# Sixteen-head attention scheduled two heads at a time, with the score matmuls of an even and an odd head alternating on the two halves of TensorE's rows

## The reference, cut to what matters

```python
def _L0_attn_b_ref(x, Q, K, V, W):
    q = jnp.einsum('qdh,bcd->bhcq', Q, x) * sq
    k = jnp.einsum('qdh,bcd->bhcq', K, x) * sq
    v = jnp.einsum('vdh,bcd->bhcv', V, x) * sv
    att = jnp.einsum('bhcq,bhCq->bhcC', q, k) / d_query
    att = jnp.where(causal, att, -jnp.inf)
    p = jax.nn.softmax(att, axis=-1)
    y = jnp.einsum('bhcC,bhCv->bhcv', p, v)
    z = jnp.einsum('dvh,bhcv->bcd', W, y) * (math.sqrt(d_embed / d_value) / num_heads)
    return z
...
x = x + _L0_attn_b_ref(_layernorm(x, axis=-1), ...)
x = x + _L0_ffn_ref(_layernorm(x, axis=-1), ...)
```

## Time and profile before

| | |
|---|---|
| time, median of 3 runs | 1553.86 us (1552.02 to 1555.83) |
| the profiled execution: its own time | 1554.59 us |
| its span | 1552.8 us |
| attention B on TensorE | about 444 to 1330 us of the span |
| TensorE busy (matmul) | 1316.0 us, 85% |
| VectorE busy | 1109.7 us, 71% |
| ScalarE busy | 952.8 us, 61% |
| GpSimd busy | 764.5 us, 49% |

### The profile page before, as it was taken

How to read it: one execution, slowest core, us unless ns; L and a number is a source line. 1 busy time by engine, 2 the same in 40 slices (tenths; PEclk the granted TensorE clock), 3 DMA queues, 4 the chain that set the end, 5 groups by cost and what they waited for, 6 DMA issues and landing times. The chain is left out here.

```text
span 1552.8 us, 28434 instructions
## 1 busy us (share of the span) xinstructions
PE 1316.0 (85%) x8377; PEld 1121.1 (72%) x8377; DVE 1109.7 (71%) x2822; ACT 952.8 (61%) x2522; POOL 764.5 (49%) x954
## 2 busy tenths in 40 slices
PE   2676744999849999999999999999999995499990
PEld 1565633888837888888888888888888884388880
DVE  5666434777727788888887888888888874377771
ACT  1555322444427788888788888888887885144440
POOL 3015362444415555576575674765765655244443
PEclk9888556999959999999999999999999997699995
DMA  9391011222100000000000000000000000122215
GB/s 182 131 355 33 25 38 44 57 58 56 36 28 14 1 15 1 2 23 7 1 25 5 5 25 1 22 8 1 11 5 5 11 1 14 37 57 58 56 44 163
DMA packets 91936, 64.47 MB, mean 42 GB/s; under 512 B 34020, under 2 KB 77935, under 8 KB 91792
## 3 DMA queue, kind: packets, MB, share of 16 engines
q1 hardware_dynamic: 83152, 45.75, 10.8%
q0 software_dynamic: 8640, 16.93, 3.4%
HBM read 26.59 MB, written 36.96 MB: 41 GB/s over the span
## 5 line engine op out<-in xcount | busy, mean ns | idle before, releaser
L1359 POOL TENSOR_TENSOR b_probs<-b_probs,b_recip 128x128 f32<-128x128 f32 (+3 forms) x512 | 352.2, 718 | 309.9 <-DVE b_recip L1592 309.9
L420 DVE TENSOR_TENSOR b_pt_lo<-b_ring,b_pt_hi 128x512 fp32r<-128x512 f32 (+1 forms) x384 | 219.0, 598 | 94.0 <-ACT b_pt_hi L414 91.7
L545 ACT ACTIVATE b_probs<-b_s_bank,b_neg_max 128x256 f32<-128x256 f32 (+3 forms) x512 | 267.8, 533 | 28.2 <-DVE b_neg_max L537 26.8
L537 DVE TENSOR_REDUCE b_neg_max<-b_s_bank 128x1 f32<-128x256 f32 (+3 forms) x512 | 219.4, 477 | 48.7 <-PE b_s_bank L529 47.7
L1219 POOL DMA_INDIRECT y_rows<-f_y_sb,f_dest x142 | 138.9, 978 | 215.1 <-DVE f_y_sb L1197 207.7
L414 ACT ACTIVATE b_pt_hi<-b_ring 128x512 fp32r<-128x512 f32 (+1 forms) x384 | 192.1, 547 | 9.6 <-PE b_ring L485 8.8
L81 PE MATMUL b_s_bank<-b_k_hi,b_q_hi 64*128 64x256 f32 (+3 forms) x512 | 180.8, 353 | 2.9 <-ACT b_probs L545 1.4
L485 PE MATMUL b_ring<-ident,b_probs 128*128 128x128 f32 x1280 | 178.6, 277 | 4.6 <-DVE b_q_lo L420 4.4
L82 PE MATMUL b_s_bank<-b_k_lo,b_q_hi 64*128 64x256 f32 (+3 forms) x512 | 164.6, 322 | 0.0
L554 PE MATMUL b_pv_bank<-b_pt_hi,b_v 128*128 128x512 f32 (+3 forms) x512 | 159.2, 322 | 6.3 <-DVE b_y L1555 5.2
L83 PE MATMUL b_s_bank<-b_k_hi,b_q_lo 64*128 64x256 f32 (+3 forms) x512 | 164.0, 320 | 0.0
(11 more groups left out here) (303 smaller groups left out, 3341.0 us busy)
## 6 DMA issues: line engine op xcount, KB each, us to landing
x_sorted<-a_blank SPq DMA_DIRECT2D x64, 260.0 KB, 3.9
f_xs<-x_sorted SPq DMA_DIRECT2D x142, 65.0 KB, 1.8
b_yc<-y_rows SPq DMA_DIRECT2D x16, 256.0 KB, 3.1
f_yc<-y_rows SPq DMA_DIRECT2D x16, 256.0 KB, 3.2
y_rows<-f_y_sb,f_dest POOLq DMA_INDIRECT x142, 2.2
x_tok<-in_L_attn_a_x_dram SPq DMA_DIRECT2D x8, 256.0 KB, 4.5
out_dram<-x_tok SPq DMA_DIRECT2D x8, 256.0 KB, 2.5
f_raw<-in_L_ffn_W_dram SPq DMA_DIRECT2D x1, 1408.0 KB, 6.6
```

The source lines that it names most:

```text
L420: nc.vector.tensor_tensor(dst, src(rg.of(key)), hi.bitcast(F32), ALU.subtract).then_inc(rg.lo_done, 1)
L537: nc.vector.tensor_reduce(sc.neg_max[:, i:i + 1], s_tile(sc, i), AX.X, ALU.max, negate=True).then_inc(sc.max_done, 1)
L545: nc.scalar.activation(probs[:, P_AT[i]:P_AT[i] + (i + 1) * P], s_tile(sc, i), ACT.Exp, bias=sc.neg_max[:, i:i + 1], accum_out=sums[:, i:i ...
L1359: nc.gpsimd.tensor_tensor(part, part, recip[:, i:i + 1].to_broadcast([P, (i + 1) * P]), ALU.mult).then_inc(probs_done, 1)
```

## The change

`attention_b` now counts slots in pairs of heads: p runs over 64 pairs, with eight slots for a sequence. What changes inside:

- **Scores** (`scores(p, group)`): three groups of tiles, (3,), (2, 0) and (1,). In each group the matmuls of the even head (x = 0, rows 0 to 63) and of the odd head (x = 1, rows 64 to 127) alternate, into two different banks of the same three banks, which are handed out round (`s_use` modulo 3). TensorE's other work of the slot stands between the groups.
- **Buffers**: `probs` has three buffers instead of two, `pt`, `neg_max`, `sums` and `recip` have two each (one for each x). To make room, `xn` uses the routing's `xn_t`, `yc` uses `xn_t` and `z`, and `over` and `spread` of the routing lie over other tiles.
- **Order**: on every engine the steps of a slot are put in a new order. The transposes of the even head of pair p − 1 stand right behind the first score group of p; those of the odd head stand before the last group. The division of both heads of p − 1 stands in slot p. The projections of q and k for p + 1 stand behind the last score group in every slot, followed by one set of products alone.
- **Waits**: the exponential of the odd head's first group waits until the even head before it has been transposed (its `probs` buffer is that head's).
- The once-a-sequence steps have new slot numbers, and GpSimd's `rstd` stands ahead of the division in its slot.

What is computed, and the shapes of all matmuls, copies and exponentials, stay as they are. The diff, cut to its core:

```diff
+P_GROUPS = ((3,), (2, 0), (1,))
+P_COL = {3: 0, 2: 0, 0: 3 * P, 1: 0}
+P_EXP = ((1, 2), (4, 6), (7, 8))
...
-    NU = NB * NH
-    SUMMED, ADDED, SEEN, NORMED, TURNED = 1, 2, 3, 4, 6
-    Z_COPY, Z_TURN, Z_ADD, MEANT, APPLIED, DOUBLED, ROWS, SCORED, RANKED, COUNTED, SENT = 3, 4, 5, 7, 8, 9, 10, 11, 12, 14, 15
-    slots = range(-1, NU + NH)
+    NQ = NB * NP
+    SUMMED, ADDED, NORMED, TURNED = 0, 1, 2, 3
+    Z_COPY, Z_TURN, MEANT, APPLIED, ROWS, COUNTED = 2, 3, 4, 5, 6, 7
+    slots = range(-1, NQ + NP)
...
+    for p in slots:
+        order += turns(p - 1, 0) if alive(p - 1) else []
+        order += [("v", p + 1)] if alive(p + 1) else []
...
+        order += turns(p - 1, 1) if alive(p - 1) else []
...
+        order += [("q", p + 1), ("k", p + 1)] if alive(p + 1) else []
...
+            def divide(p, x):
+                pool.wait_ge(recip_done, 2 * p + x + 1)
...
+                if leaving(p, APPLIED) is not None:
+                    rstd(nc, pool, g, rt.m, leaving(p, APPLIED))
+                if alive(p - 1):
+                    divide(p - 1, 0)
...
+            def scores(p, group):
+                if group == 0:
+                    pe.wait_ge(rg.lo_done, rg.lo["k", p])
+                if s_use(p, group, 1) >= 3:
+                    pe.wait_ge(exp_done, exps_before(s_use(p, group, 1) - 3))
+                tiles = P_GROUPS[group]
+                for i in tiles:
+                    for a, c in ((0, 0), (0, 1), (1, 0)):
+                        for x in range(2):
+                            rows = slice(x * KD, x * KD + KD)
+                            nc.tensor.matmul(s_at(p, group, x, i), q[a][rows, i * P:i * P + P], k[c][rows, 0:(i + 1) * P],
+                                             start=(i == tiles[0] and a + c == 0), stop=False)
...
+            def transposes(p, x):
+                pe.wait_ge(probs_done, (2 * p + x + 1) * QT)
...
+            for p in slots:
+                if alive(p):
+                    scores(p, 0)
+                if alive(p - 1):
+                    transposes(p - 1, 0)
...
+                if alive(p - 2):
+                    products(p - 2, 1)
+                if alive(p):
+                    scores(p, 1)
+                if alive(p + 1):
+                    values(p + 1)
...
+                if alive(p - 3):
+                    output(p - 3)
+                if alive(p - 1):
+                    transposes(p - 1, 1)
...
+                if alive(p):
+                    scores(p, 2)
+                if alive(p + 1):
+                    project(p + 1)
+                if alive(p - 1):
+                    products(p - 1, 0)
...
+                for x in range(2):
+                    act.wait_ge(max_done, exps_before(s_use(p, group, x)))
+                    if group == 0 and x == 1 and p > 0:
+                        ring_filled(act, rg, turns(p - 1, 0)[-1])
...
+                    split_lo(nc, dve, rg, ("q", p + 1), q[1][:], q[0][:])
+                    split_lo(nc, dve, rg, ("k", p + 1), k[1][:], k[0][:])
+                if alive(p):
+                    for x in range(2):
+                        dve.wait_ge(exp_done, exps_before(s_use(p, 2, x)))
+                        wait(dve, probs_done, (2 * p + x - 1) * QT)
+                        nc.vector.reciprocal(recip[x][:], sums[x][:]).then_inc(recip_done, 1)
+                if alive(p - 1):
+                    value(p - 1, 0)
```

More of the change, by code:

```diff
@@ L1281, in attention_b @@
         sem = lambda n: ctx.enter_context(nc.semaphore(f"b_{n}"))
-        sc = Scores(nc, ctx, "b", g)
+        s_bank = [pb(f"s_bank{i}") for i in range(3)]
         rg = Ring(nc, ctx, "b_ring", 3, order)
@@ L1370, in _ @@
+            for j in range(NK * QT):
                 route_scatter(nc, pool, g, rt, NB - 1, j)
@@ L1411, in products @@
-            def products(u):
+            def scores(p, group):
[10 more added lines that the diff above has]
+                                             start=(i == tiles[0] and a + c == 0), stop=False)
+                at = P_COL[tiles[0]] + tiles[0] * P
+                for x in range(2):
+                    nc.tensor.matmul(s_bank[s_use(p, group, x) % 3][:, at:at + len(tiles) * P], g.ident_bf[:],
+                                     g.mask[:, 0:len(tiles) * P], start=False, stop=True).then_inc(s_full, 1)
@@ new lines, in _ @@
+            for p in slots:
+                if alive(p):
+                    exponentials(p, 0)
+                if alive(p - 1):
+                    transposed(p - 1, 0)
+                if alive(p - 2):
+                    low(p - 2, 1)
+                if alive(p):
+                    exponentials(p, 1)
+                if alive(p + 1):
+                    hi, lo, bank = v_parts(p + 1)
+                    split_hi(nc, act, rg, ("v", p + 1), hi, bank)
+                if coming(p, TURNED) is not None:
+                    turned(coming(p, TURNED))
+                if leaving(p, ROWS) is not None:
+                    route_turned(nc, act, g, rt, rg, leaving(p, ROWS))
+                if alive(p - 2):
+                    act.wait_ge(y_done, 2 * p - 2)
+                    wait(act, z_full, p - 2)
+                    nc.scalar.activation(y_parts[0][:], y[:], ACT.Copy).then_inc(y_hi_done, 1)
+                if alive(p - 1):
+                    transposed(p - 1, 1)
+                if alive(p):
+                    exponentials(p, 2)
+                if alive(p + 1):
+                    split_hi(nc, act, rg, ("q", p + 1), q[0][:])
+                    split_hi(nc, act, rg, ("k", p + 1), k[0][:])
+                if leaving(p, Z_COPY) is not None:
+                    act.wait_ge(z_full, (leaving(p, Z_COPY) + 1) * NP)
+                    act.wait_ge(yc_summed, min(leaving(p, Z_COPY) + 3, NB))
+                    nc.scalar.activation(z[:], z_bank[:], ACT.Copy).then_inc(z_done, 1)
+                if coming(p, NORMED) is not None:
+                    normed(coming(p, NORMED))
+                if leaving(p, APPLIED) is not None:
+                    route_apply(nc, act, g, rt, leaving(p, APPLIED))
+                    route_double(nc, act, g, rt, leaving(p, APPLIED))
+                if alive(p - 1):
+                    low(p - 1, 0)
@@ L1545, in added, with maxima, transposed, value @@
                                         ALU.add).then_inc(x_done, 1)
+            def maxima(p, group):
+                for x in range(2):
+                    dve.wait_ge(s_full, s_use(p, group, x) + 1)
+                    for i in P_GROUPS[group]:
+                        nc.vector.tensor_reduce(neg_max[x][:, i:i + 1], s_at(p, group, x, i), AX.X, ALU.max,
+                                                negate=True).then_inc(max_done, 1)
+            def transposed(p, x):
+                for i in range(len(PT_BANKS)):
+                    head_transposed_lo(nc, dve, rg, turns(p, x), pt[x], i)
+            def value(p, x):
+                u = 2 * p + x
+                dve.wait_ge(low_done, u + 1)
+                nc.vector.tensor_tensor(y[x * KD:x * KD + KD, :], pv_bank[0:KD, :], y[x * KD:x * KD + KD, :],
+                                        ALU.add).then_inc(y_done, 1)
             summed(0)
```

360 lines of the change are left out of this document (146 added, 214 removed).

## The result

| | before | changed |
|---|---|---|
| median of the runs, us | 1553.54 (1552.02 to 1555.83, 4 runs) | 1950.03 (1944.15 to 1954.75, 4 runs) |
| the profiled execution, us | 1554.59 | 1950.79, span 1949.0 |

The changed kernel takes 1.252 times as long (95% interval 1.2494 to 1.2554), 396 us more. Forecast: 1935 us, range 1820 to 2050. What remains is which terms of the sum carried that, and what the pairs are worth.

A forecast was written before the change was run, and what follows sets the result against it. TensorE bounds attention B before, a chain of waits between engines after: 16.8 us a slot, 1.4 once-a-sequence steps, 0.8 clock, 19.0 against 13.04. Over 64 slots 381 us more than 1554.59, about 1935 us, range 1820 to 2050.

The forecast's parts named there:

- What bounds before: Attention B before the change: TensorE bounds it, busy 596.48 of 600 us, 13.04 us a pair of heads.
- The chain around a slot: Attention B: waits between engines from one low part of k to the next pair's, a floor of 16.8 us a slot.
- step 8: Chain's last step: two exponentials 0.94 us, high parts of q and k 0.50 + 0.60, low part of k 0.68; t = 16.3.
- the handovers: Chain in attention B: about ten handovers between engines of 0.05 us each, taking it from 16.3 to 16.8 us.
- `rstd` ahead of the division: GpSimd, two slots of eight: the division starts later, +4.0 us in `NORMED` and +3.3 us in `APPLIED`.
- The other once-a-sequence steps: `turned`, `added` and three `route_` steps on the chain, about 3 us, late value sums 1 us; with `rstd` 1.4 us a slot.
- The clock: TensorE in attention B: gaps lower the granted clock for part of the time, +0.8 us a slot.
- the high end: TensorE's clock low throughout attention B: about +4 us a slot, 256 us; a fifth of it was taken.
- The sum: Whole kernel: 19.0 us a slot against 13.04, 64 slots, 381 us more, about 1935 us.
- TensorE's own gain: Paired score matmuls in attention B: TensorE's work falls by 1.4 us a pair, from 13.04 to 11.6 us.
- That the gain changes TensorE's idle time only: Attention B: score matmuls end before VectorE needs them, so the 1.4 us gain or its absence isn't in the chain.
- The rival that TensorE stays the bound: Attention B: chain under 11.6 us, pairs overlap, 1465 us; needs ScalarE and VectorE to run ahead of TensorE; chance 0.03.

The follow-up runs named there:

- experiment 2: Changed kernel with both reciprocals ahead of the low parts of the next pair's q and k on VectorE: 1899.4 us, ratio 1.2207.
- experiment 3: Changed kernel with the even head's division ahead of the two `rstd` calls on GpSimd: 1885.7 us, ratio 1.2127.
- experiment 6: Changed kernel with the moves of experiment 2 and experiment 3, and `route_rank` moved behind the next slot's `maxima(p, 0)`: 1818.5 us, ratio 1.1685.
- experiment 4: Changed kernel with eight unused 512-column matmuls a slot ahead of TensorE's wait for the first division: 1946.5 us, ratio 1.2511.
- experiment 5: Changed kernel with unused 512-column matmuls in all three TensorE gaps of a slot (8, 9 and 3): 1945.9 us, ratio 1.2503.
- experiment 9: Changed kernel's matmuls, pairs and buffers in another step order, each head's transposes ahead of the exponential needing its buffer: 1492.3 us, ratio 0.9579.
- experiment 11: Changed kernel with each head's score matmuls of a group followed at once by its mask, so heads can't overlap: 1957.5 us, ratio 1.2563.
- experiment 1: Changed kernel with the even head's three passes ahead of the odd head's in each score group: 1950.0 us, ratio 1.2527.
- experiment 10: Kernel of experiment 9 with the even head's matmuls ahead of the odd head's in every score group: 1515.3 us, ratio 0.9748.
- experiment 12: Kernel of experiment 9 with each head's score matmuls of a group followed at once by its mask: 1631.4 us, ratio 1.0492.
- experiment 7: Changed kernel's matmuls, buffers and banks with the steps of all four engines in a first new order, from tables: 1629.2 us, ratio 1.0459.

## Why the prediction was right, point by point

- **What bounds before.** TensorE, as read; nothing in the runs speaks against it.
- **The chain around a slot,** 16.8 us as a floor at full clock: plain slots are 17.1 to 17.6 us, and the one at clock 1.00 throughout is 17.1. Its links are where they were put. Experiments 2, 3 and 6 took links out and the time followed (-51, -64, -132 us), in experiment 2 by half of what was expected. The figure itself holds a slip: step 8 adds 0.94 + 1.10 + 0.68 = 2.72 us to 14.05, which is 16.8 and not 16.3, and with the handovers the chain should have read 17.3 us. The plain slot of 17.1 is between the two. Added rightly, the forecast would have been some 1968 us, still in the range.
- **`rstd` ahead of the division,** +4.0 and +3.3 us in two slots of eight, which by 8 sequences is 58 us: moving it back gave 64 us (experiment 3).
- **The other once-a-sequence steps were undersized.** The term was 1.4 us a slot for all. By the slots of the sequence shown, the three long ones are 4.9, 6.2 and 5.0 us over the plain 17.1, 2.0 us a slot by themselves. The largest missing part is a step that the prediction names nowhere: `route_rank`, 3.1 us on the chain; its slot is 3.2 us shorter in experiment 6, which moves it too, and 0.5 us shorter in each of experiments 2 and 3, which don't. My 0.2 us for a small pass comes from a reciprocal; beside the divisions three of `route_rank`'s five passes took 0.51, 0.81 and 1.22 us.
- **The clock,** +0.8 us a slot as a fifth of the high end. The fifth was a choice, and the high end's own terms (1.0, 1.2 and 1.4 us) add up to 3.6 us and not 4. The direction is right (0.86), a size of 0.9 us was seen in two slots at 0.82, and filling one gap or all three (experiments 4 and 5) gained some 4 us at most. How much of the 18.4 to 19.1 us slots is clock and how much small passes stays open. Both terms together were 2.2 us over a chain of 16.8; measured, the mean slot of the sequence shown is 19.8, 2.7 over 17.1.
- **The sum.** 19.0 us a slot were forecast and 19.6 measured. By 64 slots that would be some 417 us; the time grew by 396, as the first and last slots are shorter. So the total came closer than the slot did. That it came within 15 us is luck: chain and once-a-sequence steps were both too short, and the slots at the two ends gave part of that back.
- **TensorE's own gain.** I took 1.4 us a pair, with weight loads of the two halves one after the other. It is 1.8 (2.80 us for the three groups of experiment 9 against 4.62): pairs of 128 columns start 0.06 to 0.11 us apart, so their loads overlap too. The Trainium skill says so ("TensorEngine Tiling (Array Packing)", Key Properties): different tiles can execute weight loads and matmuls in parallel; the trace agrees, and I had not used it.
- **That the gain changes TensorE's idle time only:** shown by experiment 11, some 8 us for all of it, not by experiment 1.
- **The rival that TensorE stays the bound,** 1465 us: it did not happen in this order. But the reason named against it, that the other engines can't run ahead with one buffer each for q and k, doesn't hold in general: with the same buffers experiment 9 reached 1492 us. It was the order that held them.

## What to carry to other kernels

When a change makes one engine's work cheaper and regroups the work to do so, cost the regrouping first: follow one round of waits from a step back to itself, each link by a row, and compare its length with the fullest engine's work. If the round is longer, the saving is worth nothing until the order lets steps of older items stand between those of new ones; here the same matmuls gave 1950 or 1492 us. And read in the trace whether an "undone" variant is undone before its time is taken as evidence.

## What the runs showed of the hardware

- **Matmuls on different halves of the rows pass one another,** so TensorE's starts don't follow the program's order. Three queued matmuls of one head don't hold up the other head's (experiments 1 and 10: the mask comes 0.90 us behind the first of six matmuls of 512 columns, in either order); with six ahead (three of 384 and three of 128 columns) it starts 0.45 us late, and one over all 128 rows holds it up fully (experiment 12). The Trainium skill has it otherwise ("TensorE: Matmul & The Clock Gate", The mechanism: matmuls are strictly first in, first out; by the same section it is weight loads that are pulled ahead). The group of one tile in experiment 10, where the program has three matmuls of the even head and then three of the odd one:

```profile
758.28 0.50 PE L1487 MATMUL b_s_bank<-b_k_hi,b_q_hi 64*128 64x512 f32 x2
758.59 0.43 PE L1487 MATMUL b_s_bank<-b_k_lo,b_q_hi 64*128 64x512 f32 x2
758.82 0.43 PE L1487 MATMUL b_s_bank<-b_k_hi,b_q_lo 64*128 64x512 f32 x2
759.18 0.29 PE L1491 MATMUL b_s_bank<-mask,ident_bf 128*128 128x128 bf16 x2
```

  By that rule the odd head's first could start with the even head's third at the earliest, 0.54 us in, and the mask 0.54 + 0.90 = 1.44 us in. It came after 0.90. The measurement decides.
- **Small VectorE passes beside GpSimd's divisions took 2.5 to 4.4 times as long.** Means from 600 to 1500 us, before and changed:

```profile
L683 DVE TENSOR_TENSOR b_r_apart<-b_r_scores 128x256 f32<-128x256 f32 x8 | 3.3, 418 | 0.0
L732 DVE TENSOR_TENSOR b_r_of_score<-b_r_chosen,b_r_scores 128x64 f32<-128x64 f32 x8 | 1.7, 216 | 0.0
```

```profile
L683 DVE TENSOR_TENSOR b_r_apart<-b_r_scores 128x256 f32<-128x256 f32 x5 | 5.1, 1028 | 0.0
L732 DVE TENSOR_TENSOR b_r_of_score<-b_r_chosen,b_r_scores 128x64 f32<-128x64 f32 x5 | 4.8, 952 | 0.0
```

  Behind a PSUM bank as one input no such thing shows (the value sum is 0.68 to 0.69 us in both). The Trainium skill ("SBUF — State Buffer", Who interferes with whom) describes an exclusive lock: a VectorE instruction with two SBUF inputs that meets a GpSimd instruction which reads SBUF and was there first waits for the whole of it. The trace agrees: 0.6 and 0.7 us more on average is within one division of 512 columns, 1.04 us. No run took the divisions away from beside these passes, so the cause is read from the times alone.
- **One gap's length doesn't tell whether the clock falls.** In the changed kernel it stayed at 1.00, the higher level, through gaps of 1.74, 2.90 and 2.94 us, as this stretch shows (columns as in the earlier trace rows); in experiment 7 it was at 0.50, the lower one, from 800 to 806 us behind a gap of 1.75 us.

```profile
912.00:950.00 38.00, 23.60 (x170) 18.95 (x170) 23.66 (x58) 20.62 (x58) 19.54 (x24) 1.00 0.03 8
```
